# Four projections of a step on TensorE: pairs of 64-column matmuls written as 128x128 by 256

## What is computed

```
shift = silu(causal_depthwise_conv(x, conv_w, conv_b))
rk    = shift @ in_proj_w.T            # (.., 2M): r, k = rk[..., :M], rk[..., M:]
mg    = shift @ mem_gate_w.T + mem_gate_b
sel   = softplus(mg[..., :M]);  tau = sigmoid(mg[..., M:])
k     = k / max(norm(k), 1e-12) * sel ** tau;   g = -sel * tau
u     = sigmoid(x @ w0.T @ w1.T + b1) * x
S_t   = exp(g_t) * S_{t-1} + k_t u_t;  o_t = r_t S_t / 8
y     = layernorm(x + o + shift * residual_weight)
...                                    # signs of y choose a tile per token; spline; layernorm
```

## Time and profile before

| | before |
|---|---|
| median of 3 runs (lowest, highest) | 1308.65 us (1307.91, 1309.11) |
| the profiled execution | 1311.31 us, span 1309.2 us |
| busy share PE, DVE, ACT, POOL | 89%, 81%, 73%, 64% |
| matmul records on PE, mean granted clock | 9346, 0.908 |

### The profile page before, as it was taken

How to read it: one execution, slowest core, us unless ns; L and a number is a source line. 1 busy time by engine, 2 the same in 40 slices (tenths; PEclk the granted TensorE clock), 3 DMA queues, 4 the chain that set the end, 5 groups by cost and what they waited for, 6 DMA issues and landing times. The chain is left out here.

```text
span 1309.2 us, 31773 instructions
## 1 busy us (share of the span) xinstructions
PE 1158.9 (89%) x9346; PEld 735.1 (56%) x9346; DVE 1061.5 (81%) x2508; ACT 951.7 (73%) x1809; POOL 833.4 (64%) x1692
## 2 busy tenths in 40 slices
PE   5799999999999999999999999999999965588700
PEld 4556666666666666666666666666666632333100
DVE  4888889999999999999999999998988765586710
ACT  5657888888888888888888888888888743444760
POOL 3125666767676767676767676767676665335576
PEclk9989999999999999999999999999999977655555
DMA  4112222222222222222222222222222116689993
GB/s 141 34 37 102 103 103 104 102 102 102 102 102 102 102 103 106 106 106 106 106 106 106 106 106 106 106 106 106 106 105 102 71 65 234 230 316 352 419 409 125
DMA packets 64115, 175.05 MB, mean 134 GB/s; under 512 B 11580, under 2 KB 23108, under 8 KB 64071
## 3 DMA queue, kind: packets, MB, share of 16 engines
q1 hardware_dynamic: 49430, 138.85, 28.7%
q10 hardware_dynamic: 8496, 33.56, 6.6%
q0 software_dynamic: 6144, 2.11, 1.2%
HBM read 69.06 MB, written 101.20 MB: 130 GB/s over the span
## 5 line engine op out<-in xcount | busy, mean ns | idle before, releaser
L1052 DVE SCALAR_TENSOR_TENSOR acc<-xT_all,cw_sb,acc 128x256 f32<-128x256 f32 x768 | 354.3, 520 | 7.2 <-ACT acc L751 7.1
L777 ACT ACTIVATE sg<-TX,bet,gam 128x256 f16<-128x256 f32 x256 | 129.5, 556 | 42.2 <-PE TX L464 42.2
L484 PE MATMUL PR<-xT_all,w_sb 128*128 128x256 f32 x512 | 139.1, 396 | 2.9 <-ACT xT_all L715 2.9
L1384 POOL TENSOR_TENSOR AT<-AT,Wm 128x128 f32<-128x128 f32 x224 | 114.8, 512 | 41.7 <-DVE AT L1078 25.9
L496 PE MATMUL WK<-w_sb,tS 128*128 128x512 f32 x256 | 138.3, 622 | 0.0
L751 ACT ACTIVATE acc<-xT_all,cb_sb,cw_sb 128x256 f32<-128x256 f32 x256 | 132.5, 592 | 4.8 <-DVE xT_all L1038 2.8
L538 PE MATMUL OB<-th_all,AT 128*128 128x512 f32 x256 | 124.4, 609 | 11.7 <-POOL AT L1384 10.2
L566 PE MATMUL PR<-shT,w_mg_sb 128*64 128x128 f32 x2048 | 128.0, 278 | 6.5 <-ACT shT L760 6.5
L566 PE MATMUL PR<-shT,w_rk_sb 128*64 128x128 f32 x2048 | 125.9, 276 | 0.0
L566 PEld LDWEIGHTS PR<-shT,w_rk_sb 128*64 128x64 f32 x2048 | 110.5, 137 | 26.3 <-issue 26.3
L566 PEld LDWEIGHTS PR<-shT,w_mg_sb 128*64 128x64 f32 x2048 | 112.5, 138 | 18.9 <-issue 12.0
(11 more groups left out here) (230 smaller groups left out, 2665.1 us busy)
## 6 DMA issues: line engine op xcount, KB each, us to landing
xin_all<-in_x SPq DMA_DIRECT2D x32, 1024.0 KB
y_ring<-y_all SPq DMA_DIRECT2D x32, 1024.0 KB, 4.1
y_scratch<-y_all SPq DMA_DIRECT2D x32, 1024.0 KB, 6.1
own<-y_scratch SPq DMA_DIRECT2D x5, 2048.0 KB, 16.1
out<-own ACTq DMA_DIRECT2D x5, 2048.0 KB, 19.9
rows<-y_scratch SPq DMA_DIRECT2D x4, 2048.0 KB, 12.3
out<-rows ACTq DMA_DIRECT2D x4, 2048.0 KB, 13.6
RX<-RE SPq DMA_DIRECT2D x128, 32.2 KB
```

The lines of the kernel that those rows point to most:

```text
L484: i = pe.matmul(PR[:, 0:T], w0_sb[:, blk, :], xT[b][:, blk, HIST:HIST + T], start=(blk == 0), stop=(blk == NB - 1))
L777: nc.scalar.activation(sg[:, blk, :], TX[:, (blk % 2) * T:(blk % 2 + 1) * T], ACT.Sign, scale=gam[:, blk:blk + 1], bias=bet[:, blk:blk + 1 ...
L1052: v.scalar_tensor_tensor(acc[:, blk, :], xT[b][:, blk, i:i + T], cw_sb[:, blk, i:i + 1], acc[:, blk, :], ALU.mult, ALU.add).then_inc(e_con ...
L1384: q.tensor_tensor(late, late, Wm[:, :, l, :].rearrange("p c (n h) -> p c n h", h=h), ALU.add)\
```

## The change

The projections of r and k, and those of the two gates, become one matmul of 128 columns of weights by 256 tokens. In PR the partitions are now (projection, row of M) and the columns (chunk, token). The copies out of PR put each chunk's part on its half of the partitions, so that rr, kk, ksq and xs look as before; each of them is two instructions of 64x128, one for each chunk, xs four. The bias is now one column of 128 partitions, loaded by one DMA. Readers of rr, kk and ksq wait for both instructions.

```diff
-            mb_sb = sb("mb_sb", [P, 2])
+            mb_sb = sb("mb_sb", [P, 1])
...
-            e_xs, e_kk, e_ks, e_rr, e_xa = ev("e_xs", 2), ev("e_kk"), ev("e_ks"), ev("e_rr"), ev("e_xa")
+            e_xs, e_kk, e_ks, e_rr, e_xa = ev("e_xs", 4), ev("e_kk", CPG), ev("e_ks", CPG), ev("e_rr", CPG), ev("e_xa")
...
-                    for c in range(CPG):
-                        for k in range(2):
-                            sp.dma_start(mb_sb[chunk_rows(c), k:k + 1], mem_b[k * M:(k + 1) * M, :]).then_inc(s_cw, 16)
+                    sp.dma_start(mb_sb[:], mem_b).then_inc(s_cw, 16)
...
-                    wait(pe, e_ks, k)
+                    done(pe, e_ks, k)
...
-                    for n in range(2):
-                        for blk in blocks:
-                            for c in range(CPG):
-                                i = pe.matmul(PR[chunk_rows(c), (at + n) * CH:(at + n + 1) * CH],
-                                              w[:, blk, n * M:(n + 1) * M], shT[:, blk, chunk_cols(c)],
-                                              start=(opens and n == 0 and blk == blocks[0]),
-                                              stop=(closes and n == 1 and blk == blocks[-1]))
+                    for blk in blocks:
+                        i = pe.matmul(PR[:, at * CH:(at + 2) * CH], w[:, blk, :], shT[:, blk, :],
+                                      start=(opens and blk == blocks[0]), stop=(closes and blk == blocks[-1]))
...
-                        act.wait_ge(s_cw, 112)
+                        act.wait_ge(s_cw, 64)
...
+                def projected(n, at, c):
+
+                    return PR[chunk_rows(n), (at + c) * CH:(at + c + 1) * CH]
+
...
                     for n in range(2):
-                        nc.scalar.activation(xs[:, n, :], PR[:, (2 + n) * CH:(3 + n) * CH], ACT.Identity,
-                                             bias=mb_sb[:, n:n + 1]).then_inc(e_xs.sem, 1)
+                        for c in range(CPG):
+                            nc.scalar.activation(xs[chunk_rows(c), n, :], projected(n, 2, c), ACT.Identity,
+                                                 bias=mb_sb[chunk_rows(n), :]).then_inc(e_xs.sem, 1)
...
-                    nc.scalar.activation(kk[:], PR[:, CH:2 * CH], ACT.Copy).then_inc(e_kk.sem, 1)
+                    for c in range(CPG):
+                        nc.scalar.activation(kk[chunk_rows(c), :], projected(1, 0, c), ACT.Copy).then_inc(e_kk.sem, 1)
...
-                    nc.scalar.activation(ksq[:], PR[:, CH:2 * CH], ACT.Square).then_inc(e_ks.sem, 1)
+                    for c in range(CPG):
+                        nc.scalar.activation(ksq[chunk_rows(c), :], projected(1, 0, c), ACT.Square).then_inc(e_ks.sem, 1)
...
-                    nc.scalar.activation(rr[:], PR[:, 0:CH], ACT.Copy, scale=R_SCALE).then_inc(e_rr.sem, 1)
+                    for c in range(CPG):
+                        nc.scalar.activation(rr[chunk_rows(c), :], projected(0, 0, c), ACT.Copy, scale=R_SCALE)\
+                            .then_inc(e_rr.sem, 1)
```

More of the change, by code:

```diff
@@ L989, in _ @@
                 dve.wait_ge(s_pc, 3)
-                dve.wait_ge(s_cw, 112)
+                dve.wait_ge(s_cw, 64)
                 linked = [0]
@@ L1166, in key_norm @@
                     wait(dve, e_kg, k)
-                    wait(dve, e_kk, k)
+                    done(dve, e_kk, k)
                     earlier(dve, e_KE, k, 1)
@@ L1174, in read_key @@
                     wait(dve, e_kn, k)
-                    wait(dve, e_rr, k)
+                    done(dve, e_rr, k)
                     earlier(dve, e_A, k, 1)
```

## The result

The changed kernel takes 1370.32 us (median of 4 runs, 1365.01 to 1375.3), the kernel before 1308.58 (median of 4): ratio 1.047 (95% interval 1.045 to 1.050). Forecast were 1295 us, range 1279 to 1304. The prediction was wrong in sign: 62 us slower. The profiled execution took 1370.73 us.

The account below looks back on a forecast made before the run. The prediction took PE's own work to bound the kernel, with POOL's and ACT's loop close behind. Gains of 10.6 (loop), 1.9 (start) and 1.2 (ramp) sum to 13.7 us: 1308.65 becomes 1295.0 us, range 1279 to 1304.

Parts of the forecast that it names:

- PE, 1.24 us a step: Projection blocks on PE: shorter blocks and cheaper edges save 1.24 us a step, bounds 1.0 to 1.4.
- E: Rival on PE: full-width weight loads not hidden behind matmuls, +157 us, 1460 us; chance 0.01.
- ACT, +0.98 us: Copies out of PR on ACT: ten instead of five add 0.98 us a step, bounds 0 and 2.2.
- Half the partitions cost the whole time: ACT copies: a 64-partition copy should cost as much as a 128-partition one, doubling the copies' time, 0.98 us more.
- So the copies are costed at 0; their cover is gone at 1.4 us: ACT's added 0.98 us fits within 1.42 us between the fourth tanh and PE's L525, so it costs nothing.
- D: Rival: ten ACT copies add over 2.66 us a step and PE waits at L505 or L525; 1317 or 1342 us; chance 0.12.
- POOL's step unchanged in length: Expected sign in the trace: POOL's work per step takes as long as before, change 0.
- The loop, 0.38 us a step gained: POOL's and ACT's loop takes over the pace, leaving 0.38 us of PE's 1.24 per step; 10.6 us in 28 steps.
- C: Rival: loop already closed, at most 0.1 us a step gained in the middle; 1302.8, up to 1307 us; chance 0.14.
- Start, 1.9 us: Kernel start: one DMA for mb_sb instead of four lets DVE begin 1.9 us earlier, bounds 0 and 2.5.
- The ramp: First full-rate steps: PE keeps its whole gain until the loop catches up, 1.2 us, 0 to 3.

Follow-up runs that it names:

- e4: Changed kernel plus 12 filler float32 matmuls a step that keep PE busy ahead of the wait for ksq: 1350.2 us, ratio 1.030.
- e17: Kernel before with only rr and kk each copied as two 64x128 instructions, matmuls untouched: 1318.5 us, ratio 1.007.
- e15: Changed kernel with nm made by ACT instead of POOL, and ACT's third and fourth tanh, rr, kk and ksq put ahead of xs: 1318.6 us, ratio 1.007.
- e3: Changed kernel's matmuls with the five full-width copies of before, values in wrong places: 1353.3 us, ratio 1.033.
- e5: e3 with nm made by ACT instead of POOL: 1310.2 us, ratio 0.999.
- e18: e5 with DVE's read of the key norms (nl) moved ahead of yn: 1309.3 us, ratio 0.999.
- e1: Kernel before, matmuls untouched, each of the five copies out of PR split by partitions into two of 64x128: 1374.5 us, ratio 1.048.
- e12: Kernel before with only r and k projections as 128x256 matmuls, rr, kk, ksq narrow, nm on ACT, bb ahead of a convolution round: 1327.7 us, ratio 1.012.

## Why the prediction was wrong

- **PE, 1.24 us a step: right.** Block 1.73 us, transposes 0.44; e4 gives PE's own step as 31.12 us against 31.14 worked out. The 0.09 ahead of the block is gone, which still agrees with the Trainium skill on changes of the tiling mode (TensorEngine Tiling (Array Packing), Key Properties). The loads (E) stay hidden.
- **ACT, +0.98 us: the term that was mis-sized.** It measured 2.64, above the upper bound of 2.2, which had counted the ten copies (3.34 us here against 3.2) but not that xa and the tanh between them lose their overlap too (0.28). "Half the partitions cost the whole time" held for the duration. The overlap with the neighbour did not. The Trainium skill (ScalarE: Activation LUTs, What ACT_TABLE_LOAD costs) gives some 93 ns of overlap between ACTIVATEs of 128 partitions; the trace agrees there, and at 64 partitions shows none.
- **"So the copies are costed at 0; their cover is gone at 1.4 us": the step that failed.** It asked who waits behind the copies, named PE's L505 and L525 and ACT's own work, and worked out the room of L525 alone. It did not follow ACT's own work on to its reader on PE: L552 had 0.71 us of room behind keT_sb. Nor did it see that in every second step the loop's end stands behind L525, with 0.58 us of room. e17 shows it: 0.88 us, well under the claimed cover, costs 9 us. In the changed kernel PE waits 1.05 us for ksq, 0.07 for the fourth tanh, and 0.41 for keT_sb or 0.47 at the loop's end. e15 shows that nearly all is saved if the copies are put behind what waits.
- **The clock was no part of the sum.** D priced PE's wait at its length. In most steps a wait of 1.05 us was followed by a stretch at half clock; e4 returns 20 us by keeping PE busy. By D's own arithmetic 2.64 us would break even (2.66). They cost 62 us because the waits at keT_sb and at the loop's end are not in it (0.8 us a step with those ahead of them, net of PE's gain) and neither is the clock (1.3 us a step, read from the trace).
- **"POOL's step unchanged in length": wrong.** With PE's gain alone, nm was held up by DVE's run (e3, +42 us). In the changed kernel this is rare (3.9 us in 2 of 64, 454 ns on average), so the two losses don't add.
- **The loop, 0.38 us a step gained: that another loop takes over was right, the gain was not.** PE does come to wait for the other engines, but at 32.4 to 32.5 us a step (e5, e18), not 32.0, which is no gain over 32.38; C, with at most 0.1 us a step, was nearer. Three places were loosened (bb; bb, nl and history; the key norms) and each time the next wait came up at the same length. Which instruction I over-credited in the loop is not settled.
- **Start, 1.9 us: 0.85 measured.** Behind the loads the next late thing is POOL's mask. The ramp wasn't measured apart.
- **Rival D** named the right copies and one right place, at 0.12, and its times (1317, 1342) were too low for want of these waits and the clock. (At 0.4 us a copy its terms give +7 us and not +8.)

## What to carry to other kernels

Cover is the smallest slack among all readers of everything behind the lengthened instruction, on every engine: for each reader, take the time from the end of what it needs to its own start, also where it does not wait yet and has no bracket. PE's L552 had none. The end of a loop body behind a waiting instruction is a reader too. Where three engines are busy for 80 to 100% of the time, a shorter matmul block is worth nothing until the loop behind it is measured, and it shifts other work against each other. If an engine's instructions must become longer, put them behind what others wait for before giving up the change: that was worth 52 us here, together with nm on ACT. Halving an ACT copy by columns was nearly free, halving it by partitions doubled it and cost the overlap.

## What the runs showed of the hardware

- ACT on 64 partitions: 0.27 us (0.36 with the bias), the next starts 0.03 us behind the end, on the same half or across (e1, changed kernel); on 128 partitions by 64 columns two take 0.34.
- A 128x1 product on POOL took 3.90 us under a gapless run of DVE instructions with two SBUF inputs, and ended with it.
- The granted clock fell from 2.4 to 1.2 GHz for a part of 18 of 25 steps of the changed kernel, each time directly behind a wait of PE of 1.05 us (twice of 1.6); behind other waits of the same 1.05 it stayed. It fell in 4 of 25 steps where the longest wait was 0.82 us (e1), and in 4 of 25 where it was 0.5 (e12). Twelve filler matmuls a step kept it at 1.00 (e4).
- Where the last waiting matmul of the loop body (L525) was held up by the fourth tanh, the first matmul of the next pass started 0.84 to 0.94 us behind the end of that tanh (e1, e17, changed kernel).
